# One attention and expert layer on one core: the first block's maxima added by a picker matmul, the loads reordered, the last block's parts subtracted on TensorE

## What is computed

```python
c_kv = x @ W_dkv.T                                   # 2048 x 64
q    = (x @ W_dq.T @ W_uq.T).reshape(B, T, 16, 8)
k_eff = (W_dq.T @ W_uq.T @ W_uk).reshape(16, 8, 64)
v_eff = transpose((W_uv.T @ W_o.T).reshape(64, 16, 8), (1, 0, 2))
attn = softmax(causal((q . k_eff) . c_kv / sqrt(8)))
y    = (attn . c_kv) . v_eff
x = layernorm(x + y)
x = layernorm(x + experts(x))      # 8 experts, top 2, capacity 80 in each of 2 halves of the tokens
```

## Time and profile before

| what | value |
|---|---|
| median of the runs | 602.5 us (602.09 to 602.53) |
| profiled execution, its own time | 608.68 us |
| its span, first to last instruction | 606.9 us |
| mean granted TensorE clock | 0.944 |
| TensorE matmuls busy | 531.1 us (88%) |
| VectorE busy | 448.1 us (74%) |
| ScalarE busy | 350.5 us (58%) |
| GpSimd busy | 63.1 us (10%) |

### The profile page before, as it was taken

The page is one execution under the profiler, slowest core; times in us unless marked ns, Lnnn a source line. Parts: engine busy times, 40 slices in busy tenths (PEclk is TensorE's granted clock), DMA queues, the critical chain, the costliest instruction groups (busy, mean ns, idle before and its releaser), DMA issues.

```text
span 606.9 us, 10348 instructions
## 1 busy us (share of the span) xinstructions
PE 531.1 (88%) x3444; PEld 222.1 (37%) x3491; DVE 448.1 (74%) x1311; ACT 350.5 (58%) x751; POOL 63.1 (10%) x64
## 2 busy tenths in 40 slices
PE   4976999889999997989989999899999988937990
PEld 2523433333333333235444333232232221223990
DVE  4796999798898988857768888788888804259326
ACT  0614566656776764756646776568767788710220
POOL 9300000000000000720001700000000000000050
PEclk9967999999999999989999999899999999976975
DMA  3489894100000300110000420000000000000041
GB/s 85 129 209 190 204 263 113 22 1 2 3 1 2 78 2 2 53 39 2 12 2 18 51 15 1 1 2 1 2 2 0 2 2 18 18 0 1 11 47 36
DMA packets 25410, 24.90 MB, mean 41 GB/s; under 512 B 2314, under 2 KB 22668, under 8 KB 25356
## 3 DMA queue, kind: packets, MB, share of 16 engines
q1 hardware_dynamic: 21660, 20.42, 14.0%
q0 software_dynamic: 1280, 2.62, 3.5%
q10 hardware_dynamic: 2416, 1.18, 0.7%
HBM read 16.81 MB, written 7.28 MB: 40 GB/s over the span
## 4 chain that ended last, share of the span: by engine, by line
PE 55%; issue 21%; DVE 13%; ACT 4%; DMA 3%; POOL 3%; SPq 0%; ACTq 0%; DVEq 0%; POOLq 0%
PE acc L1058 15%; PE sc L1020 15%; PE scT L1041 11%; DVE part_max L749 3%; POOL exp_in L551 2%; DVE unused L754 2%; ACT probs L629 2%; PE sc L1136 2%; PE scT L1045 2%; DMA qT<-maxT 1%; PE ms L1143 1%; PE ms L1149 1%; DVE kT L909 1%; DMA wo<-in_L_attn_W_dkv 1%; DVE x L822 1%
## 5 line engine op out<-in xcount | busy, mean ns | idle before, releaser
L629 ACT ACTIVATE probs<-scT 128x512 f32<-128x512 f32 (+3 forms) x640 | 304.9, 537 | 145.5 <-PE scT L1045 80.8
L749 DVE TENSOR_REDUCE part_max<-sc 128x1 f32<-128x512 f32 x384 | 254.4, 685 | 47.2 <-PE sc L1020 44.4
L1020 PE MATMUL sc<-kT,qT 126*128 126x512 bf16 (+3 forms) x640 | 221.6, 360 | 13.3 <-DVE part_max L749 5.4
L1041 PE MATMUL scT<-qT,kT 128*128 128x512 bf16 (+3 forms) x593 | 201.1, 350 | 5.7 <-ACT probs L629 5.2
L1058 PE MATMUL acc<-probs,v 128*9 128x512 f32 (+3 forms) x1280 | 147.8, 534 | 0.7
L754 DVE CUSTOM_DVE_ANT_0 unused<-sc,causal 128x128 bf16<-128x128 f32 (+3 forms) x256 | 120.2, 483 | 21.4 <-PE sc L1020 19.3
L1020 PEld LDWEIGHTS sc<-kT,qT 126*128 126x128 bf16 x640 | 61.9, 98 | 178.8 <-DVE part_max L749 102.6
L1041 PEld LDWEIGHTS scT<-qT,kT 128*128 128x128 bf16 x640 | 62.0, 99 | 58.1 <-ACT probs L629 33.0
L1045 PE MATMUL scT<-later,ident 128*128 128x128 bf16 x256 | 55.6, 220 | 4.3 <-DMA qT<-maxT 3.8
L1058 PEld LDWEIGHTS acc<-probs,v 128*9 128x9 f32 x1280 | 19.0, 88 | 47.8 <-issue 26.1
L1045 PEld LDWEIGHTS scT<-later,ident 128*128 128x128 bf16 x256 | 25.6, 100 | 19.6 <-issue 0.3
(11 more groups left out here) (182 smaller groups left out, 341.4 us busy)
## 6 DMA issues: line engine op xcount, KB each, us to landing
kT<-parts_k SPq DMA_DIRECT2D x9, 384.0 KB
qT<-parts_q SPq DMA_DIRECT2D x9, 384.0 KB
wi<-in_L_ffn_wi SPq DMA_DIRECT2D x1, 2048.0 KB, 19.0
parts_k<-wi SPq DMA_DIRECT2D x3, 384.0 KB, 3.8
parts_q<-wi SPq DMA_DIRECT2D x3, 384.0 KB, 5.1
kT<-parts_k SPq DMA_DIRECT2D x12, 96.0 KB
qT<-parts_q SPq DMA_DIRECT2D x12, 96.0 KB
x<-in_L_attn_x ACTq DMA_DIRECT2D x4, 256.0 KB, 4.3
```

What stands on the lines that cost most here:

```text
L629: nc.scalar.activation(probs[n % PRING][:, 0:width], scT[n % SRING][:, 0:width], ACT.Exp).then_inc(exp_done, 1)
L749: nc.vector.tensor_reduce(dst, sc[i % SRING][:, :], AX.X, ALU.max).then_inc(sc_used, 1)
L1020: nc.tensor.matmul(sc[i % SRING][:, 0:w], qT[s % 2][0:MROW, head, qt * P:(qt + 1) * P], kT[0:MROW, head, c * QUERIES:c * QUERIES + w], sta ...
L1041: ins = nc.tensor.matmul(scT[n % SRING][:, 0:QUERIES - off], kT[:, head, j * P:(j + 1) * P], qT[s % 2][:, head, off:QUERIES], start=True, ...
```

## The change

- Weights are split over two queues: SP issues wuq, wdq, wdkv and then x blocks 0 and 2; ScalarE's queue issues wo, wuk, wuv, then x blocks 1 and 3 and the router.
- For units of block 0 no DMA brings the maxima to qT. maxT gets 128 rows (8 used, the rest zero), and `scores` adds the maxima with a second matmul of 128 rows against `pick16[:, h, :]`, which has ones in the two rows of head h and zeros elsewhere. POOL makes pick16, minus16 (the negative identity) and zeroes maxT, five instructions ahead of the fills of kT.
- Block 3 (the last 512 tokens) is no longer projected ahead of the first maxima. TensorE does it between the first twelve: two projections into acc and scT[0], and the split by matmuls of minus16 with a part, added into the same bank, so that ScalarE copies all three parts from the banks and VectorE has no part in it. VectorE clears acc after `max_rows(0)`.
- EARLY is 0, the lead is 2 steps for units 0 to 3, 3 for unit 4 and 5 for the others, RUSH_WORK is 3300. By the same planner steps 0 to 5 then have 10, 6, 0, 10, 6 and 10 items instead of 2, 9, 5, 8, 6 and 6; 32 items are done after step 1, 64 after step 6 and 143 after step 18.

```diff
-EARLY = 16
-LEAD = 5
+EARLY = 0
+LEADS = [2] * GROUPS + [3] + [5] * (UNITS - GROUPS - 1)
-RUSH, RUSH_WORK = 20, 3000
+RUSH, RUSH_WORK = 20, 3300
 def max_step(u):
-    return max(0, FIRST[u] - LEAD - 1)
+    return max(0, FIRST[u] - LEADS[u] - 1)
...
         @block.sync
-            for dst, src in ((wuq, wuq_d), (wuk, wuk_d), (wo, wo_d), (wdq, wdq_d), (wuv, wuv_d), (wdkv, wdkv_d)):
+            for dst, src in ((wuq, wuq_d), (wdq, wdq_d), (wdkv, wdkv_d)):
                 sp.dma_start(dst, src).then_inc(s_w, 16)
+            for i in range(0, SUPERS, 2):
+                sp.dma_start(x[:, i * QT:(i + 1) * QT, :], token_rows(x_d, i * QT, (i + 1) * QT)).then_inc(s_x[i], 16)
...
         @block.gpsimd
+            nc.gpsimd.tensor_scalar(minus16[:, :], ident16[:, :], -1.0, None, ALU.mult).then_inc(picked, 1)
+            nc.gpsimd.memset(pick16, 0.0).then_inc(picked, 1)
+            for m in maxT:
+                nc.gpsimd.memset(m[:, :], 0.0).then_inc(picked, 1)
+            pool.wait_ge(picked, 4)
+            nc.gpsimd.tensor_tensor(pick16[0:2 * HG, :, :], ident16[0:2 * HG, 0:HG].unsqueeze(2).to_broadcast([2 * HG, HG, P]),
+                                    ident16[0:2 * HG, HG:2 * HG].unsqueeze(2).to_broadcast([2 * HG, HG, P]), ALU.add).then_inc(picked, 1)
...
         @block.scalar
-            for i in range(SUPERS):
+            for dst, src in ((wo, wo_d), (wuk, wuk_d), (wuv, wuv_d)):
+                act.dma_start(dst, src).then_inc(s_w, 16)
+            for i in range(1, SUPERS, 2):
                 act.dma_start(x[:, i * QT:(i + 1) * QT, :], token_rows(x_d, i * QT, (i + 1) * QT)).then_inc(s_x[i], 16)
...
-                    act.wait_ge(kq_r1, k + 1)
-                    nc.scalar.activation(split[2 * (i % SPLITS) + n][:, 1, :], rest[n], ACT.Copy).then_inc(kq_mid, 1)
+                    act.wait_ge(*((less_hi, n + 1) if last else (kq_r1, k + 1)))
+                    nc.scalar.activation(split[2 * (i % SPLITS) + n][:, 1, :], kq_banks(i)[n][:, :] if last else rest[n], ACT.Copy).then_inc(kq_mid, 1)
+                for n in range(2 if last else 0):
+                    act.wait_ge(less_mid, n + 1)
+                    nc.scalar.activation(split[2 * (i % SPLITS) + n][:, 2, :], kq_banks(i)[n][:, :], ACT.Copy).then_inc(lo_last, 1)
...
             def max_to_rows(u):
+                if super_of(u) == 0:
+                    return
...
         @block.vector
-            for i in range(SUPERS):
-                if i + 1 < SUPERS:
-                    keep_xT(i + 1)
+            for i in range(SUPERS - 1):
+                keep_xT(i + 1)
...
                 max_rows(u)
+
+            dve.wait_ge(lo_last, 1)
+            nc.vector.memset(acc[:, :], 0.0).then_inc(s_const_v, 1)
...
         @block.tensor
+            def subtract(n, part, kept, done):
+                pe.wait_ge(kept, 2 * (SUPERS - 1) + n + 1)
+                nc.tensor.matmul(kq_banks(SUPERS - 1)[n][:, :], minus16[:, :], split[2 * ((SUPERS - 1) % SPLITS) + n][:, part, :],
+                                 start=False, stop=True, skip_group_check=True).then_inc(done, 1)
...
                 if j == 0 and h == 0:
-                    pe.wait_ge(max_in[u % 2], 16 * (u // 2 + 1))
+                    if s:
+                        pe.wait_ge(max_in[u % 2], 16 * rows_sent(u))
+                    else:
+                        pe.wait_ge(maxT_kept, u + 1)
...
+                if s == 0:
+                    nc.tensor.matmul(scT[n % SRING][:, 0:QUERIES - off], pick16[:, h, :], maxT[u % 2][:, off:QUERIES],
+                                     start=False, stop=True, skip_group_check=True)
...
+            scores_for_max(0)
+            scores_for_max(1)
+            project(SUPERS - 1, 0)
+            scores_for_max(2)
+            scores_for_max(3)
+            project(SUPERS - 1, 1)
+            scores_for_max(4)
+            scores_for_max(5)
+            subtract(0, 0, kq_hi, less_hi)
+            scores_for_max(6)
+            scores_for_max(7)
+            subtract(1, 0, kq_hi, less_hi)
+            values(SUPERS - 1)
+            scores_for_max(8)
+            scores_for_max(9)
+            subtract(0, 1, kq_mid, less_mid)
+            scores_for_max(10)
+            scores_for_max(11)
+            subtract(1, 1, kq_mid, less_mid)
+            for i in range(12, ITEMS_BEFORE[AHEAD]):
+                scores_for_max(i)
+            turn_max(0, ms[:, :]).then_inc(w_made, 1)
```

More of the change, by code:

```diff
@@ L108, in max_step, with rows_sent @@
 def max_step(u):
-    return max(0, FIRST[u] - LEAD - 1)
+    return max(0, FIRST[u] - LEADS[u] - 1)
+def rows_sent(u):
+    return max(0, len(range(u % 2, u + 1, 2)) - len(range(u % 2, GROUPS, 2)))
 def item_work(i):
@@ L286, in program @@
         tri16 = sb("tri16", [P, P], BF16)
+        minus16 = sb("minus16", [P, P], BF16)
         later16 = sb("later16", [P, P], BF16)
@@ L295, in program @@
         max16 = [sb(f"max16_{i}", [P, QT, 2, HG], BF16) for i in range(2)]
-        maxT = [sb(f"maxT{i}", [2 * HG, QUERIES], BF16) for i in range(2)]
+        maxT = [sb(f"maxT{i}", [P, QUERIES], BF16) for i in range(2)]
         recip = sb("recip", [P, HEADS, 1])
@@ L325, in program @@
         x1T = einT[:, 0:QUERIES]
+        pick16 = einT[:, 0:HG * P // 2].bitcast(BF16).rearrange("p (h k) -> p h k", h=HG)
         hT = [sb(f"hT{i}", [P, FC, CAP]) for i in range(2)]
@@ L342, in program @@
         s_const_v = sem("s_const_v")
+        picked = sem("picked")
+        less_hi = sem("less_hi")
+        less_mid = sem("less_mid")
+        lo_last = sem("lo_last")
         s_rows = sem("s_rows")
@@ L403, in kq_banks @@
         def kq_banks(i):
+            if i == SUPERS - 1:
+                return (acc, scT[0])
             return (sc[0], sc[1]) if i % 2 == 0 else (acc, ms)
@@ L433, in store_parts @@
                 sp.wait_ge(kq_mid, 2 * i + n + 1)
-                sp.wait_ge(kq_lo, 2 * i + n + 1)
+                sp.wait_ge(*((kq_lo, 2 * i + n + 1) if i < SUPERS - 1 else (lo_last, n + 1)))
                 for first in range(0, COPIES[n], PARTS):
@@ L589, in _ @@
             for i in range(SUPERS):
+                last = i == SUPERS - 1
                 for n in range(2):
@@ L605, in keep_maxT @@
             def keep_maxT(u, bank):
-                if u >= 2:
-                    act.wait_ge(max_in[u % 2], 16 * (u // 2))
-                nc.scalar.activation(maxT[u % 2][:, :], bank.bitcast(BF16)[0:2 * HG, 0:QUERIES], ACT.Copy).then_inc(maxT_kept, 1)
+                if 2 <= u < GROUPS + 2:
+                    act.wait_ge(scT_made, HG * FIRST[u - 1])
+                elif u >= 2:
+                    act.wait_ge(max_in[u % 2], 16 * rows_sent(u - 2))
+                nc.scalar.activation(maxT[u % 2][0:2 * HG, :], bank.bitcast(BF16)[0:2 * HG, 0:QUERIES], ACT.Copy).then_inc(maxT_kept, 1)
             def max_to_rows(u):
+                if super_of(u) == 0:
+                    return
                 act.wait_ge(maxT_kept, u + 1)
                 g = u % GROUPS
-                act.dma_start(qT[super_of(u) % 2][MROW:MROW + 2, g * HG:(g + 1) * HG, :], maxT[u % 2][:, :]).then_inc(max_in[u % 2], 16)
+                act.dma_start(qT[super_of(u) % 2][MROW:MROW + 2, g * HG:(g + 1) * HG, :], maxT[u % 2][0:2 * HG, :]).then_inc(max_in[u % 2], 16)
             for u in range(AHEAD):
@@ L738, in _ @@
                     nc.vector.tensor_tensor(parts[n][:, 2, :], rest[n], parts[n][:, 1, :], ALU.subtract).then_inc(kq_lo, 1)
-            dve.wait_ge(kq_r1, 2 * SUPERS)
-            nc.vector.memset(acc[:, :], 0.0).then_inc(s_const_v, 1)
             def row_max(i):
@@ L991, in _, with project, values @@
             pe.wait_ge(w_kept, 8)
[L992 to L999, removed]
+            def project(i, n):
+                nc.tensor.matmul(kq_banks(i)[n][:, :], (kw, qw)[n], xT[:, i * QUERIES:(i + 1) * QUERIES], start=True, stop=True).then_inc(kq_made, 1)
+            def values(i):
                 if i:
@@ L1005, in _ @@
                 ins.then_inc(v_made, 1)
+            def subtract(n, part, kept, done):
+                pe.wait_ge(kept, 2 * (SUPERS - 1) + n + 1)
+                nc.tensor.matmul(kq_banks(SUPERS - 1)[n][:, :], minus16[:, :], split[2 * ((SUPERS - 1) % SPLITS) + n][:, part, :],
+                                 start=False, stop=True, skip_group_check=True).then_inc(done, 1)
+            for i in range(SUPERS - 1):
+                pe.wait_ge(xT_kept, i + 1)
+                for n in range(2):
+                    if i >= 2:
+                        pe.wait_ge(kq_r1, 2 * (i - 2) + n + 1)
+                    project(i, n)
+                values(i)
                 if i + 2 < SUPERS:
@@ L1065, in _ @@
             pe.wait_ge(s_const, 9)
[L1066 to L1073, removed]
+            pe.wait_ge(picked, 5)
+            pe.wait_ge(xT_kept, SUPERS)
+            scores_for_max(0)
[20 more added lines that the diff above has]
+            turn_max(0, ms[:, :]).then_inc(w_made, 1)
```

(1 more changed line is left out.)

## The result

The changed kernel takes 605.23 us (median of 12 runs, 603.79 to 606.73) against 602.51 of the kernel before beside it (12 runs): ratio 1.0043, 95% interval 1.0024 to 1.0061. It is slower by 2.7 us, where I forecast 1.9 faster. The range held it; the sign was wrong.

A forecast was written before the change was run, and what follows sets the result against it. VectorE's maxima bound the kernel until step 18, TensorE after. Earlier start and late tokens cancel; the dropped transfer, less new idle, brings step 18 to 107.2 from 109.07: 602.5 - 1.9 = 600.6 us; own range 599.5 to 601.3, eight-in-ten 597.0 to 605.5.

The forecast's parts named there:

- What bounds: Whole run: VectorE's maxima pace 50.57 to 109.07 us, TensorE's unchanged work the rest; only when step 18 is reached matters.
- Weights first: Front: weights on two queues let transposes begin at 6.2 us, moving first scores 2.6 us earlier, 30.36 to 27.8.
- POOL's instructions: Ahead of the fills of kT: five new instructions take 1 to 3 us in all, costed at nothing because covered.
- The last 512 tokens: First 16 maxima: start at 28.1, 4.0 us lost to TensorE's added work, end 39.1; cancels the earlier start.
- The choice of the low clock: First maxima: low clock assumed after TensorE's empty stretch, 4.0 us lost; at full clock 2.3.
- No transfer for block 0: Ahead of step 0: next maximum at 41.45 after the turn, no wait on a transfer; step 18 through at 107.2.
- Rival E: Ahead of step 0: transfer normally hidden, so the 3.06 us pause is not there to win; 603.7 us, chance 0.06.
- idle time of VectorE from the 17th to the 143rd maximum: Steps 0 to 18: 3.72 less 1.26 (low clock) plus 0.8 (step 2) plus 0.9 (picks), 4.2 us.
- Picks: Steps 0 to 17: 64 pick matmuls take 8.8 us of TensorE, mostly hidden by VectorE's pace; 0.9 us charged.
- C: Step 0: low clock stays, 1.26 idle kept, picks 0.9 more, 602.8; or x block 0 late, 601.5; chance 0.22.
- D: Steps 0 to 17: TensorE becomes the bound, step 18 at 110.8, 604.2 us; sign VectorE idle over 6; chance 0.20.
- Group 4's transfer: Maxima still sent, three steps ahead instead of five, 9.8 us against 8.51; cost 0, at most 2 us.

The follow-up runs named there:

- e6: Changed kernel with 16 maxima ahead of step 0 again, its short leads and limit of 3300 kept; 604.43 us (one execution).
- e12: Changed kernel with idle matmuls ahead of the later waits, after step 18; 602.99 us, ratio 0.9973 to the kernel before.
- e8: Changed kernel with idle matmuls around the first scores and ahead of step 0, to hold the clock full; 604.67 us (one execution).
- e5: Changed kernel with the plan of before (16 maxima ahead of step 0, lead 5, limit 3000); 602.96 us, ratio 1.0019 to the kernel before.
- e4: Kernel before with the picker alone (pick matmuls, no transfer of maxima for block 0), old plan; 603.96 us, ratio 1.0004.
- e13: Changed kernel with the plan of before and idle matmuls ahead of the later waits; 598.94 us, ratio 0.9911 to the kernel before.
- e14: Changed kernel, own plan, with idle matmuls at the start to hold the clock and ahead of the later waits; 601.31 us, ratio 0.9960.
- e1: Kernel before, unchanged, run again for a second profile; 604.54 us (one execution).
- e7: Changed kernel with each pick matmul made twice with halves, the sum the same; 613.57 us (one execution).
- e2: Kernel before with the weights-first loads alone; 602.51 us, ratio 0.9983 to the kernel before.
- e11: Kernel before with idle matmuls ahead of the later waits, after step 18; 599.37 us, ratio 0.9893 to the kernel before.
- e10: e9 with idle matmuls ahead of five waits long after the change; 597.61 us, ratio 0.9914 to the kernel before.
- e9: Kernel before with new loads and picker, old plan, without the late tokens' change; 602.09 us, ratio 1.000 to the kernel before.

## Why the prediction was wrong

- **What bounds.** Right that VectorE's maxima up to the 143rd decide between the two plans. Not right that the rest is the same time for both: 489 to 498 us in the profiles, by clock falls that come in some executions.
- **Weights first.** Right in the mechanism: first matmul 4.87, transposes at 6.72 (forecast 6.2), first scores 27.78 (forecast 27.8); alone, the 143rd 2.3 earlier. That the scores came on the forecast with the transposes 0.5 late is luck: first scores stand at 29.6 to 30.4 in the profiles with the old loads and at 27.6 to 28.6 with the new, a gain nearer 2 than 2.6. POOL's instructions push the fills of kT from 3.62 to 6.65, the upper end of the 1 to 3 us estimated, and cost nothing that shows: the first scores wait for the load of the products, as before.
- **The last 512 tokens.** Right for this execution: pauses 4.0 us, end of the first maxima 39.3 (forecast 39.1). The choice of the low clock was luck: in e6 and e12, with the same instructions up to there, the clock was full, the pauses 1.6 (forecast 2.3) and the end at 37.2 and 37.1. Alone, 1.4 later at the 143rd (the sum had 2.6).
- **No transfer for block 0.** The turn was right, 41.68 for 41.45. Rival E fell, the pause is real. The first exponential came at 42.74 (forecast 41.8).
- **The step that failed is the idle time of VectorE from the 17th to the 143rd maximum: I put it at 4.2, it is 9.3** (71.35 us less 62.09 of work; busy 0.87, where I named over nine tenths as the sign). I let the 1.26 of the low clock go and added 0.8 for step 2 and 0.9 for picks. In its place: 3.5 us from the 17th to the 33rd, where I had 0.8. Of these, 2.3 go when the clock is held (e8); it had fallen again after 36.0 to 40.5, where TensorE was busy 1.92 of 4.50 us (3.69 in e8, which keeps the full clock). The other 1.25 are nearly all the wait for group 1's turn. And 5.7 us from the 33rd on, all at full clock, where I had 3.7 less 1.26 plus 0.9.
- **The plan.** I moved 16 maxima from ahead of step 0 into it at the price of their own work. Ahead of step 0 they ran without a gap, during the turn and the transfer, although the clock was low: a cover that the change gave up together with the transfer it covered. In the new place two turns lie open, and the low clock, which ahead of step 0 cost these maxima nothing, slows them from 6.98 to 9.48. With the picker and the old plan (e5, e4) the cover stays, the pause is gone too, and it is worth 2.4 us against the new plan with the clock held (e13 against e14) and 4.05 against it without (e13 against e12).
- **Picks.** 0.9 of 8.8 was too little: the picker alone lengthens the 33rd to 143rd by 2.3 (e4), VectorE idles 1.8 us longer there in e4 than in e1 without a low step 0 that e1 still has, and e7's second set cost 5.1.
- **Rivals C and D came together.** C's condition, a low clock in step 0, held, and D's sign as well: VectorE idle over 6 us, TensorE busy 11.12 of 11.16 and 56.39 of 60.19. I had priced the two together at 606, and 605.23 came; D alone, at 110.8 for the 143rd, lies between my 107.2 and the 113.0 seen. e7's shortfall from 8.8 says TensorE does not set the pace alone.
- **Group 4's transfer** is not waited for: right.

Not tried: a plan made for the picker, between the two seen here.

## What to carry to other kernels

Work that filled a wait is part of what the wait costs: if the wait is taken away, look at what the same work was covering besides. Here the 16 maxima ran almost as fast in their new place at full clock, but two turns lay open and a fall of the clock reached them. Time put on an engine just below its neighbour's load can come through: of 8.8 us of picks here 5.1 did (e7). Where runs scatter by one per cent, compare landmarks inside the traces before the totals, choose two landmarks between which equal kernels agree, and look for what the time after them does.

## What had not been expected of the hardware

The granted clock fell behind the same waits of 1.9 us (near 388) and 2.6 to 2.8 us (near 266) in some executions and not in others (0.79 against 1.00 over 8 us around 266). Of the eleven profiles without idle matmuls there, nine show the fall near 266 and six the one near 388; the changed kernel and e2 show neither. In the five kernels with idle matmuls ahead of these waits, the profiles show no fall there; in three of them (e11, e12, e14) there is none from 110 to 540 us, in e10 and e13 only one in the last 4 us of that stretch. With them the kernel before went from 604.45 to 599.37 and e9 from 602.09 to 597.61, although they add work. Why e11's six runs still lie 9.7 us apart stays open.
